# Gate logits as eight extra columns of two matmul products in a ViT block, and a bias fold taken from TensorE

## What is computed

```
h  = patches(x) @ W.T + b                              # 768 -> 256
h  = h + ssm(layernorm(h))                             # 256 states, a scan over the tokens, then C and D
x2 = layernorm(h)
y1 = LN(x2 + MHA(x2), g1, be1)                         # 4 heads; attention is over the 64 images,
                                                       # q, k, v = x2 @ w.T + b; o @ ow.T + ob
gates = softmax(y1 @ wg)                               # 8 experts
idx = argmax(gates); keep the first S/8 tokens of each expert
moe = gate * ((y1 @ w1[e] + b1[e]) @ w2[e] + b2[e])    # 0 where a token isn't kept
out = h + LN(y1 + moe, g2, be2)
```

## Time and profile before

| | us |
|---|---|
| median of 3 runs | 1353.25 (1352.43 to 1354.72) |
| the profiled execution, its own time | 1356.27 |
| its span | 1354.4 |
| PE busy, share of the span | 1261.2, 93% |
| DVE busy | 1020.7, 75% |
| ACT busy | 737.2, 54% |
| POOL busy | 718.3, 53% |

### The profile page before, as it was taken

One profiled execution on the slowest core, in us unless ns is written; L12 is line 12 of the kernel. 1 busy time (PEld: TensorE's weight loads), 2 busy tenths in 40 slices (PEclk: granted clock), 3 DMA queues, 4 the chain that ended last, 5 costly groups with the idle time before them and its releaser, 6 DMA issues. The chain is left out here.

```text
span 1354.4 us, 37450 instructions
## 1 busy us (share of the span) xinstructions
PE 1261.2 (93%) x11810; PEld 1147.7 (85%) x11811; DVE 1020.7 (75%) x2787; ACT 737.2 (54%) x1515; POOL 718.3 (53%) x966
## 2 busy tenths in 40 slices
PE   2999999999999999589999999999999984999995
PEld 1999999999999999489999999999999983666663
DVE  4577778887777787747777777777777765699997
ACT  3455555555555555445555555555555541477775
POOL 1655666666656665303444444444444443277776
PEclk9999999999999999889999999999999985999998
DMA  7435454545454543202223322332223224677773
GB/s 235 147 121 168 149 163 132 163 137 178 145 182 117 178 117 98 96 28 83 96 93 101 101 93 96 99 99 95 93 97 101 97 79 133 183 215 234 226 230 121
DMA packets 97044, 180.07 MB, mean 133 GB/s; under 512 B 12319, under 2 KB 62497, under 8 KB 95970
## 3 DMA queue, kind: packets, MB, share of 16 engines
q1 hardware_dynamic: 82244, 138.66, 34.1%
q0 software_dynamic: 13312, 39.75, 8.0%
q10 hardware_dynamic: 1440, 1.07, 0.3%
HBM read 112.69 MB, written 67.80 MB: 133 GB/s over the span
## 5 line engine op out<-in xcount | busy, mean ns | idle before, releaser
L476 POOL TENSOR_TENSOR xl<-xf,xh 128x512 fp32r<-128x512 f32 x141 | 179.2, 1299 | 204.6 <-ACT xh L402 204.6
L297 PE MATMUL ps_h<-wh,xh 128*128 128x256 f32 x588 | 166.3, 283 | 4.9 <-DVE xl L611 4.9
L297 PE MATMUL ps_h<-wh,xl 128*128 128x256 f32 x588 | 166.2, 283 | 0.0
L297 PE MATMUL ps_h<-wl,xh 128*128 128x256 f32 x588 | 166.0, 282 | 0.0
L851 ACT ACTIVATE zn<-z,nm_z,rs_z 128x256 f32<-128x256 f32 x98 | 53.6, 594 | 200.7 <-DVE nm_z L982 200.7
L1323 POOL DMA_INDIRECT out<-res,c_idx x106 | 116.5, 1099 | 61.6 <-issue 46.2
L920 POOL DMA_INDIRECT bins<-rows,slot_i x98 | 100.7, 1028 | 60.1 <-POOL slot_i L914 45.2
L1471 PE MATMUL c_ps_y<-w,yt 128*128 x424 | 116.9, 398 | 6.5 <-issue 4.1
L297 PEld LDWEIGHTS ps_h<-wh,xh 128*128 128x128 f32 x588 | 111.8, 190 | 5.7 <-DVE xl L611 5.7
L297 PE MATMUL b<-x2h,wh 128*128 128x256 f32 x392 | 114.7, 293 | 0.0
L297 PEld LDWEIGHTS ps_h<-wl,xh 128*128 128x128 f32 x588 | 111.7, 190 | 0.0
(11 more groups left out here) (255 smaller groups left out, 4409.4 us busy)
## 6 DMA issues: line engine op xcount, KB each, us to landing
xf<-xt SPq DMA_DIRECT2D x49, 768.0 KB, 5.3
row<-bins SPq DMA_DIRECT2D x106, 257.5 KB
h_dram<-h1b SPq DMA_DIRECT2D x49, 256.0 KB, 5.3
x_dram<-x2o SPq DMA_DIRECT2D x49, 256.0 KB, 5.4
x<-x_dram SPq DMA_DIRECT2D x98, 128.0 KB, 2.8
rows<-h_dram SPq DMA_DIRECT2D x98, 128.0 KB, 2.8
w1s<-w1t SPq DMA_DIRECT2D x8, 1024.0 KB, 6.8
w2s<-w SPq DMA_DIRECT2D x8, 516.0 KB, 5.4
```

Of the source, the lines that this page charges most:

```text
L297: last = nc.tensor.matmul(out_ps, a, b, start=(i == 0), stop=(i == len(terms) - 1))
L476: last = nc.gpsimd.tensor_tensor(xl[:, p, part], xf[:, p, part], xh[:, p, part].bitcast(F32), ALU.subtract)
```

## The change

1. **Bias fold.** b1[e] @ w2[e] is no longer eight fp32 matmuls on PE. In slots 2 to 5 DVE adds up two products each (`sum_bias`: a column of b1 by a 128x256 part of w2, onto `acc`), and one fp32 matmul with ones (`fold_sum`, in slot 0) sums over the partitions. `b1p` and its copy on POOL are gone. SP's reloads of w2 wait for `acc_done`.
2. **Gate logits.** With t = x2 + o @ ow.T + ob and LN(t) = (t - mean) * rstd * g1 + be1, the logits are rstd * (t @ gg - mean * sum(gg)) + be1 @ wg, with gg = g1 * wg. So `w_in` and `w_o` get eight more columns each (gg and ow.T @ gg), and `values` and `project` write 264 columns instead of 256. `turn_y`, `y1t_out` and `gate` are gone. New are `xg_out` (ACT, 128x16), `add_const` (POOL), `gate_sum` (DVE), `centre` (POOL, two operations) and `logits` (DVE, two), all on 128x16 or less. The new columns are made at the end of stage A (`gate_weights` on DVE, eight transposes and ten small fp32 matmuls on PE).
3. **Norm's shift.** The second half of `y1` (adding be1 to 128x512) is moved from DVE to POOL; `scaled` is what stays on DVE.
4. **Order.** All five lists of stage B are written in another order, with `values` and `scores` one group later than `queries` and `keys`.
5. The split of the folded biases (`b12s`) is moved from DVE to POOL, ahead of POOL's steps. The semaphores of stage A are given back by one instruction and a meeting of all engines ahead of stage B.

```diff
-                        else:
-                            last = nc.tensor.matmul(ps_fb[:], b1p[:, f, :], w2s[:, f * D:(f + 1) * D],
-                                                    start=(f == 0), stop=(f == FK - 1))
...
+                def fold_sum(k):
+                    if k.slot(FOLD) == 0 and k.back(1).valid(FOLD * NE):
+                        e = k.turn(FOLD) - 1
+                        wait(pe, acc_done, (e + 1) * FK)
+                        wait(pe, fb_out, e)
+                        nc.tensor.matmul(ps_fb[:], ones_2[:], acc[:], start=True, stop=True).then_inc(fb_ps, 1)
...
+                        for f in range((k.slot(FOLD) - 2) * 2, (k.slot(FOLD) - 1) * 2):
+                            w, b = w2s[:, f * D:(f + 1) * D], w2s[:, FK * D + f:FK * D + f + 1]
+                            if f == 0:
+                                v.tensor_scalar(acc[:], w, b, None, ALU.mult).then_inc(acc_done, 1)
+                            else:
+                                wait(dve, acc_done, e * FK + f)
+                                v.scalar_tensor_tensor(acc[:], w, b, acc[:], ALU.mult, ALU.add).then_inc(acc_done, 1)
```

```diff
 # PE, stage B
                 def values(m):
                     wait(pe, Q["x2lo"], m.n() + 1)
                     wait(pe, Q["v_out"], m.n())
+                    wait(pe, Q["xg"], m.n())
+                    wait(pe, Q["sub"], m.n())
...
                 def project(m):
                     wait(pe, Q["o_lo"], m.n() + 1)
-                    wait(pe, Q["y1T"], m.n())
+                    wait(pe, Q["pos"], m.n() - 1)
                     wait(pe, Q["z"], m.n())
+                    wait(pe, Q["lg"], m.n())
...
-                    for m, stage in ((k, values), (k.back(2), turn_o), (k, queries), (k, keys), (k.back(3), turn_y),
-                                     (k.back(-1), turn_x), (k.back(1), turn_e), (k.back(3), gate),
-                                     (k.back(2), project), (k, scores), (k.back(1), attend), (k.back(3), rank)):
+                    for m, stage in ((k.back(1), values), (k, turn_x), (k.back(2), turn_e), (k.back(3), project),
+                                     (k.back(2), attend), (k, queries), (k.back(4), rank), (k.back(1), scores),
+                                     (k.back(2), turn_o), (k, keys)):
 # POOL, stage B
+                def y1(m):
+                    p = m.slot(2)
+                    wait(pool, Q["zg"], m.n() + 1)
+                    wait(pool, scattered[p], m.turn(2) * 32)
+                    g.tensor_tensor(rows[:, p, :, 0:D], zg[:], r_be1.unsqueeze(1).to_broadcast([P, 2, D]),
+                                    ALU.add).then_inc(Q["y1"], 1)
...
+                def centre(m):
+                    wait(pool, Q["zmv"], m.n() * 2 + 2)
+                    g.tensor_tensor(tm[:], mv_z[:, :, 0:1].to_broadcast([P, 2, NE]),
+                                    g_sum.unsqueeze(1).to_broadcast([P, 2, NE]), ALU.mult).then_inc(Q["tm"], 1)
+                    wait(pool, Q["tm"], m.n() + 1)
+                    wait(pool, Q["lg"], m.n() + 1)
+                    wait(pool, Q["logit"], m.n() * 2)
+                    g.tensor_tensor(dz[:], lg[:], tm[:], ALU.subtract).then_inc(Q["dz"], 1)
...
-                    for m, stage in ((k.back(4), count), (k.back(4), send), (k, add_bias), (k.back(2), rstd)):
+                    for m, stage in ((k.back(3), y1), (k.back(1), add_const), (k, add_bias), (k.back(3), count),
+                                     (k.back(2), rstd), (k.back(2), centre), (k.back(3), send)):
 # DVE, stage B
+                def logits(m):
+                    wait(dve, Q["dz"], m.n() + 1)
+                    wait(dve, Q["zrs"], m.n() + 1)
+                    wait(dve, Q["dlog"], m.n())
+                    for s in range(2):
+                        v.scalar_tensor_tensor(logit[:, s, :], dz[:, s, :], rs_z[:, s:s + 1], g_be1, ALU.mult,
+                                               ALU.add).then_inc(Q["logit"], 1)
...
-                    for m, stage in ((k.back(2), o_norm), (k.back(3), shift), (k.back(1), softmax), (k.back(3), y1),
-                                     (k.back(2), o_lo), (k.back(4), place), (k.back(-1), x_lo),
-                                     (k.back(3), top_logit), (k.back(3), expert), (k.back(2), residual),
-                                     (k.back(3), gates), (k.back(2), mean)):
+                    for m, stage in ((k.back(5), gates), (k.back(3), o_lo), (k.back(4), logits), (k.back(4), top_logit),
+                                     (k.back(4), expert), (k.back(4), scaled), (k, x_lo), (k.back(3), residual),
+                                     (k.back(3), mean), (k.back(3), gate_sum), (k.back(2), o_norm), (k.back(4), place),
+                                     (k.back(1), softmax), (k.back(3), shift)):
 # ACT, stage B
-                    for m, stage in ((k.back(3), z_norm), (k.back(2), o_hi), (k.back(1), exps), (k, v_out),
-                                     (k, lambda m: qk_out(m, "q_ps", q, 0, "q_out")),
-                                     (k.back(3), y1t_out), (k, lambda m: qk_out(m, "k_ps", kk, FT, "k_out")),
-                                     (k.back(-1), x_hi), (k.back(1), et_out), (k.back(3), e_log)):
+                    for m, stage in ((k.back(2), v_out), (k.back(2), xg_out), (k.back(5), e_log),
+                                     (k.back(2), lambda m: qk_out(m, "k_ps", kk, FT, "k_out")),
+                                     (k.back(1), lambda m: qk_out(m, "q_ps", q, 0, "q_out")), (k.back(3), o_hi),
+                                     (k.back(2), exps), (k.back(4), z_norm), (k, x_hi), (k.back(2), et_out)):
```

More of the change, by code:

```diff
@@ L129, in build @@
         c_eps = sb("c_eps", [P, 1])
+        sums = sb("gate_sums", [P, 3, NE])
+        g_sum, g_be1, g_bo = (sums[:, i, :] for i in range(3))
+        ones_2 = sb("ones_2", [P, 2])
         before = sb("before", [P, P], BF16)
@@ L618, in step @@
                 def step(k):
-                    for m, stage in ((k.back(5), scale_x), (k.back(5), shift_x), (k.back(3), of(scan, 0)),
+                    for m, stage in ((k, sum_bias), (k.back(5), scale_x), (k.back(5), shift_x), (k.back(3), of(scan, 0)),
                                      (k.back(3), of(scan, 1)), (k.back(4), residual), (k.back(1), scale_h),
@@ L684, in fold @@
                         wait(pe, w2_loaded, (e + 1) * 16)
-                    if k.slot(FOLD) == 4:
-                        wait(pe, fb_out, e)
-                        wait(pe, b1_pair, e + 1)
-                    for f in range(again * FK // 2, (again + 1) * FK // 2):
-                        if part < FT:
+                    if part < FT:
+                        for f in range(again * FK // 2, (again + 1) * FK // 2):
                             last = nc.tensor.matmul(ps_f[:, part * D:(part + 1) * D],
@@ L1175, in attend @@
                     last.then_inc(Q["av_ps"], 1)
-                def turn_y(m):
-                    wait(pe, Q["y1"], m.n() + 1)
-                    wait(pe, Q["z"], m.n() + 1)
-                    p = m.slot(2)
-                    turn(b_0, lambda s, t: rows[:, p, s, t * P:(t + 1) * P], 0).then_inc(Q["y1T_ps"], 1)
                 def turn_o(m):
```

271 lines of the change are left out of this document (183 added, 88 removed).

## The result

The changed kernel takes 1287.59 us, the median of four runs (1285.87 to 1290.78), against 1352.95 us for the kernel before in the same rounds: a ratio of 0.952, 95% interval 0.950 to 0.954, or 65 us faster. The forecast was 1269 us, with 1252 to 1296 as its range. The profiled execution of the changed kernel took 1285.87 us, that of the kernel before 1356.27 us; between these two there are 70.4 us, and the traces account for those. The changed kernel was timed only in these four executions; the kernels of the experiments were timed in later rounds, each against the kernel before in its own rounds. One of the six timed executions of split_head took 6407 us, in the chip's slow state, and is left out of its ratio; all others are fast ones.

The account below looks back on a forecast made before the run. PE was taken as the bound, busy all the time in stages A and B. Stage A -24, stage B's steps -56, its head +3 and its tail -7 sum to -84 us, giving 1269 us, range 1252 to 1296.

Parts of the forecast that it names:

- a step of B is over 9.8 us: Stage B: one of two stated signs that the forecast is wrong; the forecast step was 9.60 us.
- Stage A: Bias fold: PE's balance -28.2 us, plus 4 us for DVE's slip, gives -24 us, bounds -28 and -14.
- the 32.2: Stage A: 16 steps without bias matmuls lose 2.01 us each on PE, 32.2 us.
- The matmul with ones: Stage A: one added fp32 matmul in each block on PE, 0.50 us each, 4.0 us.
- The slip of DVE: Stage A, slots 5 and 0: DVE's sums make `sl` late for `outputs`, charged 0.5 us a block, 4 us.
- The step of stage B: Stage B: PE's step goes from 10.85 to 9.60 us, over 45 steps -56 us, bounds -56 and -43.
- Rival 1: Stage B: POOL or DVE becomes the bound, 10.2 us a step, gain 29 instead of 56, 1296 us; chance 0.17.
- Head of stage B: Stage B's start: gate weights, meeting, `x2l` and POOL's split (18 us) give +3 us altogether, bounds -2 and +10.
- The other terms: Head of stage B: `gate_weights` and the meeting +3 to +4 us, `x2l` no longer held by DVE's split -4.5 us.
- Tail: End of stage B: shorter chain of the last groups, 40.85 us becomes about 34, -7 us, bounds -3 and -11.
- Stage C: Stage C: claimed unchanged, no time gained or lost.
- The port: SBUF port shared by DVE and POOL: could hold DVE's sums in stage A, 21 us of DVE; not charged.

Follow-up runs that it names:

- split_head: Changed kernel with POOL's split of b12 in one piece in step 1 of stage B, behind `x2b` and ahead of `xg2`; ratio 0.942 to the kernel before.
- sums_only: Kernel before with only the first part of the change, the bias fold, and nothing of the gate; ratio 0.977 to the kernel before.
- padded: Changed kernel with 480 unused columns behind each of `wh` and `wl` and 488 behind `gate_sums`, moving later tensors' addresses; 1276.76 us, ratio 0.943 to the kernel before.
- shift_dve: Changed kernel with the addition of be1 moved back from POOL to DVE; ratio 0.956 to the kernel before.
- waits_more: Changed kernel with four more copies of the wait for `xg` in `scores` on PE; ratio 0.958 to the kernel before.

## Why the prediction was right, and where its steps were off

The forecast said 84 us less, the profiled executions gave 70. The range held the median with some luck, because the misses had both signs; by my own sign of being wrong ("a step of B is over 9.8 us") the forecast failed.

- **Stage A, right in the sum and wrong in its parts.** Slots 4 and 5 gave 31.5 us of the 32.2. The matmul with ones is mis-sized: it adds 0.72 us to slot 0 (11.40 - 10.68) where I took 0.50, and 0.9 in the last block, 6.0 us in all instead of 4.0. The slip of DVE is there, but smaller than the 4 us that I charged: about 1.6 us in the longer slots 5 and 0 (9.33 and 11.69), and it reaches PE through ACT's `u`, not through `sl`. The two errors cancel, which is luck. The 30.5 and 30.9 us of sums_only and padded don't show a better balance of PE: both contain the pace of 0.113 us, which the kernel before and the changed one don't have, and for which my sum had no term. Whether the kernel before could have it too, no run shows.
- **The step of stage B, 9.60 us forecast.** It is 9.70 with constant waits, 9.88 in the loop. The first 0.10 us are mis-sized terms: I let every piece that stays keep its own length, but `scores` takes 1.08 us in the new order (613.50 to 614.58) and took 0.98 in the old, `rank` up to the start of the next piece takes 0.21 (outside the loop) and took 0.14, and only `turn_e` is shorter, by 0.11. The other 0.18 us in 40 steps, 7 us, is a step left out: I compared engines and chains of data, and never priced PE's own waits. Five waits of `rank` and five of `scores`, with computed values, stand over five matmuls that are 0.12 us long together. The kernel before pays for its loop as well, 10.85 us inside against 10.73 outside. My sum started from the 10.85 and so had 0.12 us of it inside, unseen. Of the 1.25 us a step that I forecast, the change gives 1.02 outside the loops and 0.97 inside, so the loop is the smaller part of what the gain lacks. Rival 1 (POOL or DVE bound) had the direction of it and the wrong mechanism: unrolling PE alone took the 0.18 us away, and shift_dve showed that DVE's and POOL's loads were near, not over.
- **Head of stage B, +3 forecast, +12 measured.** The mechanism was right, down to `turn_x` of group 2 behind the split. The term was mis-sized: the split takes 22.3 us where I took 18 of a range of 16 to 25, and I let its lateness count once. It is 8.16 us of wait instead of 4, and 8.5 us at half the clock behind it. The other terms, -1 us together, came near: without the split in the way the whole place takes 59.0 us (split_head) against 59.2 before. One of them was too large: I took off 4.5 of the 5.53 us wait for `x2l`, and two waits of 1.41 us are left, at 554.40 and 562.31. Of the Trainium skill's statement that I had cited, GPSIMD Engine Reference, Engine selection (one-input work at roughly line rate, two-input work about half of that), the trace agrees for the cast, 1.88 us against 4.51 for two tensors. It doesn't for the two multiplications by a column, 5.45 and 5.43 us: one tensor in, and slower than with two.
- **Tail, -7 forecast, -12 measured** from `turn_o` of group 46 on; just beyond the bound of -11. Some 2 us of it are the step's own gain, since this column begins two steps ahead of the last group. That the rest is the chain without transposes and `gate` fits, but no run takes the tail apart.
- **Stage C, 0 forecast, -2.7 measured.** It is within what unchanged code shows from trace to trace.
- **The port.** I didn't charge for sums on DVE beside POOL's additions, and from 100 to 500 us there was nothing to charge: 0.48 us each. Only in the first block, while the stages fill, are some of them held: the pair at 57.27 takes 1.88 us.

## What to carry to other kernels

Work that is taken off a busy engine and put "where nothing waits" has a place in that engine's queue, and what stands behind it there may be what releases a transfer: put the one-off work behind the operations that free buffers, and check that they don't themselves wait. Count an engine's own waits as work when they stand ahead of short instructions, above all in a loop where each needs a computed value. And after adding columns to a buffer, compare the pace of steps that were not changed, also with the addresses of an earlier version: here the same instructions with the tensors at other addresses are 6.6 us shorter in one stage.

## What the runs showed of the hardware

- The place of tensors in SBUF changed the pace of PE's products at full clock: with the same instructions and other addresses it is 0.113 instead of 0.118 us a matmul in two of the six slots, and stage A takes 474.9 us instead of 481.5 (padded and the changed kernel). The mechanism stays open.
- On PE, each of four added waits on a value computed in a register cost 0.055 us in a loop, behind 0.12 us of small matmuls (waits_more, steps of 10.10 against 9.88 us); one on a constant about 0.015 us (9.77 against 9.70).
- GpSimd on 2x2048 values: cast 1.88 us, two tensors 4.51 us, one tensor by a per-partition column 5.43 to 5.45 us (the changed kernel).
